# Attention head of an eight-stage kernel: the rotary halves change places by a matmul instead of DMAs, unit 1 is stacked later, key 0's parts are made on VectorE

## What is computed

```python
cq = _gelu(x @ wq + bq)
q_c = cq @ wqc + bqc
q_r = x @ wqr + bqr
ckv = _gelu(x @ wkv + bkv)
k_r = x @ wkr + bkr
k_c = ckv @ wkc + bkc
v = (ckv @ wv + bv)...
# x is the layer-normalised input; _apply_rope on q_r and k_r:
x1, x2 = (x[..., :d // 2], x[..., d // 2:])
rot = jnp.concatenate([-x2, x1], axis=-1)
return x * cos + rot * sin
...
q = _gelu(jnp.concatenate([q_c, q_r], axis=-1))...
k = _gelu(jnp.concatenate([k_c, k_r], axis=-1))...
scores = jnp.einsum('bhqd,bhkd->bhqk', q, k) * scale
...
attn = jax.nn.softmax(scores, axis=-1)
out = jnp.einsum('bhqk,bhkd->bhqd', attn, v)
return out @ wo + bo
```

## Time and profile before

| | |
|---|---|
| median of 3 runs | 4913.53 us (4904.8 to 4913.81) |
| the profiled execution | 4910.68 us |
| its span, first to last instruction | 4908.9 us |
| PE / DVE / ACT / POOL busy | 3882.5 / 2842.9 / 2210.7 / 2466.1 us |
| mean granted TensorE clock | 0.89 |
| the attention stage's head | about 3660 to 3910 us |
| attention's main loop | about 3910 to 4500 us |
| DMAs of the swap (s_crossed) | 16 of 256 KB, median 4.4 (query) and 3.7 us (key) from issue to landing |

### The profile page before, as it was taken

The page is one execution under the profiler, slowest core; times in us unless marked ns, Lnnn a source line. Parts: engine busy times, 40 slices in busy tenths (PEclk is TensorE's granted clock), DMA queues, the critical chain, the costliest instruction groups (busy, mean ns, idle before and its releaser), DMA issues.

```text
span 4908.9 us, 49219 instructions
## 1 busy us (share of the span) xinstructions
PE 3882.5 (79%) x15176; PEld 2243.6 (46%) x15178; DVE 2842.9 (58%) x4909; ACT 2210.7 (45%) x4071; POOL 2466.1 (50%) x2147
## 2 busy tenths in 40 slices
PE   6788888759956888797788869986875798888892
PEld 2333333347743556576334336654662233334571
DVE  5999999951126675211689952227333677664522
ACT  5665666521127775111566533333343355555241
POOL 5999999922212234211799944432455412222256
PEclk9999999959978999898789979996986699998896
DMA  5555655522210010221455521124156323321144
GB/s 154 159 160 162 160 155 160 154 72 75 101 54 17 18 35 27 96 95 63 136 162 159 150 92 45 45 71 125 57 151 129 108 41 45 45 32 55 39 141 132
DMA packets 311640, 476.06 MB, mean 97 GB/s; under 512 B 34762, under 2 KB 167606, under 8 KB 311306
## 3 DMA queue, kind: packets, MB, share of 16 engines
q1 hardware_dynamic: 276864, 388.61, 29.1%
q0 software_dynamic: 28992, 75.72, 5.4%
q10 hardware_dynamic: 5504, 8.39, 0.6%
HBM read 374.87 MB, written 97.10 MB: 96 GB/s over the span
## 4 chain that ended last, share of the span: by engine, by line
PE 37%; DVE 8%; issue 4%; ACT 4%; POOL 4%; DMA 3%; SPq 0%; DVEq 0%; ACTq 0%; POOLq 0%
PE s_gate_up L2325 8%; PE s_result_sum L2341 4%; PE s_hidden_sum L1761 3%; PE s_result_sum L1772 3%; PE s_out_sum L3696 3%; PE s_shared L2981 2%; PE s_scores L3637 2%; PE s_scores_T L3680 2%; DVE s_maxima L3328 2%; DVE s_decay L370 2%; PE s_shared L2991 1%; POOL s_gathered L1047 1%; PE s_transposed L2315 1%; PE s_mid_transposed L2334 1%; DVE s_h L377 1%
## 5 line engine op out<-in xcount | busy, mean ns | idle before, releaser
L435 POOL TENSOR_TENSOR s_h<-s_dtu,s_bc 128x1024 f32<-128x1024 f32 x384 | 902.5, 2359 | 48.9 <-PE s_y_sum L477 37.1
L477 PE MATMUL s_y_sum<-s_h,identity 128*128 128x512 f32 x1536 | 763.9, 635 | 133.4 <-POOL s_h L444 121.2
L402 ACT ACTIVATE s_decay<-s_dt,s_A 128x512 f32<-128x512 f32 x768 | 498.4, 682 | 309.1 <-DVE s_h L377 302.1
L477 PEld LDWEIGHTS s_y_sum<-s_h,identity 128*128 128x128 f32 x1536 | 292.8, 201 | 570.5 <-issue 291.0
L2325 PE MATMUL s_gate_up<-s_w_gate_up,s_rowsT 128*128 x1168 | 414.8, 487 | 1.7 <-issue 1.5
L3502 ACT ACTIVATE s_weights_T<-s_scores_T 128x1024 f32<-128x1024 f32 (+3 forms) x384 | 292.6, 811 | 260.0 <-PE s_scores_T L3680 258.3
L3328 DVE TENSOR_REDUCE s_maxima<-s_scores 128x1 f32<-128x512 f32 (+3 forms) x463 | 296.5, 658 | 187.2 <-PE s_scores L3641 104.3
L444 POOL TENSOR_TENSOR s_h<-s_h,s_bc 128x512 f32<-128x512 f32 x288 | 365.8, 1271 | 17.1 <-DVE s_h L370 12.4
L2384 DVE TENSOR_TENSOR s_mid<-s_act,s_gate_up 128x128 f32<-128x128 f32 (+1 forms) x225 | 91.5, 407 | 445.7 <-ACT s_act L2357 445.7
L3550 POOL TENSOR_SCALAR_AFFINE_SELECT s_weights_T<-s_weights_T 128x256 f32<-128x256 f32 x256 | 102.7, 406 | 472.2 <-ACT s_weights_T L3502 469.5
L370 DVE TENSOR_TENSOR_SCAN s_decay<-s_decay,s_carry,s_h 128x512 f32<-128x512 f32 x240 | 302.7, 1275 | 15.8 <-ACT s_decay L402 11.5
(11 more groups left out here) (533 smaller groups left out, 7644.7 us busy)
## 6 DMA issues: line engine op xcount, KB each, us to landing
s_bc<-s_bc_rows SPq DMA_DIRECT2D x384, 512.0 KB, 5.2
sorted_results<-s_result SPq DMA_DIRECT2D x158, 128.0 KB, 2.2
s_w_inter<-in_L_ffn_experts_inter SPq DMA_DIRECT2D x16, 1024.0 KB, 5.0
s_w_exp_out<-in_L_ffn_experts_out SPq DMA_DIRECT2D x16, 1024.0 KB, 7.9
s_queries<-parts_of_q SPq DMA_DIRECT2D x96, 128.0 KB, 4.9
s_keys<-parts_of_k SPq DMA_DIRECT2D x96, 128.0 KB, 8.0
results_by_token<-zeros SPq DMA_DIRECT2D x16, 512.0 KB, 5.9
s_pair<-results_by_token SPq DMA_DIRECT2D x16, 512.0 KB
```

The costliest lines, as they stand in the source:

```text
L402: S.e.activation(self.decay[:, (2 * g + d) % 4, :], dt[q // self.passes % 2][:, at, :], ACT.Exp, scale=A[:, at, g % ns:g % ns + 1]).then_i ...
L435: G.e.tensor_tensor(self.h[r][:], dtu[q // self.passes % 2][:, at:at + 2, :], mid(self.bc[r][:, 0, :], 2), ALU.mult).then_inc(*self.fed.up())
L477: made = T.e.matmul(self.y[:, d, :], ident[:], self.h[r][:, d, :], start=False, stop=g % ns == ns - 1)
```

## The change

- **Swap.** The DMAs on `crossed` are gone. A 128x128 matrix `halves`, the identity with its halves of columns exchanged, is written once by ScalarE into the tile of zeros, which nobody reads any more by then. A new step `change` on TensorE multiplies act1 by it, 512 columns at a time, into banks 3 and 4 of PSUM, and `cross` reads its crossed operand from there. Since these banks are also those of the transposes, a transpose waits for the crossing products (`crossed_made`) and the swap of a key for the copies of the transposes.
- **Ticks.** `CROSS` for the query moves from 35 to 36, the query's gelu from 39 to 40; in `cross` the sine products come before the cosine product.
- **Parts.** VectorE takes key 0 (`(0, 1)`) besides query 1, GpSimd keeps two of four activations.
- **Stacking.** Unit 1's halves are stacked after batch 1's and batch 2's stores.

```diff
-    w_c = H.sb("w_c", [P, P])
+    w_c, halves = H.sb("w_c", [P, P]), K.zeros[:, 0:P]
...
-    act_sum, rope_sum, roped, swapped = *K.events(3), K.event(32, "dma")
-    v_step, rope_added, values_sum, value_here = K.events(4)
+    act_sum, rope_sum, roped, swapped, halves_made = K.events(5)
+    v_step, crossed_made, rope_added, values_sum, value_here = K.events(5)
...
-    ROTATE, ROTATED, CROSS, ROTARY_MADE = ((28, 30), (36, 38)), ((29, 31), (37, 39)), (35, 43), (39, 47)
+    ROTATE, ROTATED, CHANGE = ((28, 30), (36, 38)), ((29, 31), (37, 39)), (33, 40)
+    CROSS, ROTARY_MADE = (36, 43), (40, 47)
...
-    turn_bank, latent_bank = lambda k: 3 + k, 5
+    turn_bank, latent_bank, crossed_bank = lambda k: 3 + k, 5, lambda c: 3 + c
...
-                if b == 0:
+                if ct == 0 and b == 0:
                     for a in range(2):
-                        stack(ct, a)
+                        stack(0, a)
+            if b in (1, 2):
+                stack(1, b - 1)
...
                 V.wait_ge(*weights_here.now())
-                V.wait_ge(*swapped.at(2 * b + j))
-                for i, (to, table) in enumerate(((act[1][j], cos), (crossed, sin))):
-                    V.e.tensor_tensor(to[:], to[:], table[:], ALU.mult).then_inc(*v_step.up())
-                    yield PERIOD * b + CROSS[j] + i + 1
+                for c in range(CPB):
+                    V.wait_ge(*swapped.at(4 * b + 2 * j + c))
+                    V.e.tensor_tensor(crossed[:, c * CH:(c + 1) * CH], bank[crossed_bank(c)], sin[:, c * CH:(c + 1) * CH],
+                                      ALU.mult).then_inc(*crossed_made.up())
+                yield PERIOD * b + CROSS[j] + 1
+                V.e.tensor_tensor(act[1][j][:], act[1][j][:], cos[:], ALU.mult).then_inc(*v_step.up())
+                yield PERIOD * b + CROSS[j] + 2
+                V.wait_ge(*crossed_made.now())
                 V.wait_ge(*v_step.now())
...
-            if (ct, j) != (1, 0):
+            if (ct, j) not in ((0, 1), (1, 0)):
                 return
...
+            for half in (HALF["q"], HALF["k"]):
+                made = S.e.activation(halves[:, half], K.ident[:, HALF["k" if half == HALF["q"] else "q"]], ACT.Copy)
+            made.then_inc(*halves_made.up())
...
-                S.wait_ge(*roped.now())
-                S.wait_ge(*rope_added.at(2 * b + j - 1))
-                for half in range(2):
-                    S.e.dma_start(crossed[half * DC:(half + 1) * DC, :],
-                                  act[1][j][(1 - half) * DC:(2 - half) * DC, :]).then_inc(*swapped.dma())
...
-            if (ct, j) == (1, 0):
+            if (ct, j) in ((0, 1), (1, 0)):
                 return
...
+        def change(b):
+            for j in range(2):
+                yield PERIOD * b + CHANGE[j]
+                T.wait_ge(*halves_made.at(0))
+                for c in range(CPB):
+                    T.wait_ge(*roped.at(4 * b + 2 * j + c))
+                    f = take(crossed_bank(c), crossed_made.at(4 * b + 2 * j + c))
+                    T.e.matmul(f, halves[:], act[1][j][:, c * CH:(c + 1) * CH], start=True, stop=True).then_inc(*swapped.up())
```

More of the change, by code:

```diff
@@ L3182, in head @@
             work += [(n, b) for n in ("gathers", "sums", "stats", "factors", "norm", "turn", "turned_rows", "latents",
-                                      "content", "rotate", "cross", "rotary")]
+                                      "content", "rotate", "change", "cross", "rotary")]
             work += [("split", (b, ct, j)) for ct in range(DT) for j in range(2)]
@@ L3723, in main @@
                 beside(2 * s + 1)
-        head(setup=setup, turn=turn, latents=latents, content=content, rotate=rotate, maxima=maxima, highest=highest,
+        head(setup=setup, turn=turn, latents=latents, content=content, rotate=rotate, change=change, maxima=maxima, highest=highest,
              values=values)
```

## The result

The change makes the kernel faster. Median of five runs 4881.41 us (4879.5 to 4889.6) against 4913.53 us (4904.69 to 4913.93, five runs); the ratio of the times is 0.9945, 95% interval 0.9934 to 0.9957, or 27 us of 4913.5. The medians lie further apart, 32.1 us, because two of the five runs before came at 4905 us and three at 4914; the means are 27.5 apart.

What follows compares the result with a forecast made beforehand. The head was taken as bound by a chain round ScalarE, GpSimd and VectorE, beside DMA waits. Terms -13.7 +0.5 -3.0 +1.1 +0.4 = -14.7 from 4910.7 gave 4896 us, range 4882 to 4908.

Steps and rivals of the forecast that it cites:

- Batch 0, query half: Attention's head: VectorE's aggregate no longer waits for the swap, so ScalarE's normalisation comes 4.3 us earlier.
- Batch 0, key half: Swapping matmuls replace the DMA wait; aggregate 1.9 us earlier at the low clock, 6.2 for batch 0 together.
- Loads 13.7 us earlier, store of query 1 landing 13.7 earlier: Unit 0's loads start earlier through key 0 on VectorE; store duration unchanged; 13.7 us, batch 0's 6.2 contained.
- its other road: Batch 1: ScalarE's cast reached through the add waiting for gathered rows, not query 1's store; ready near 3755.
- Batch 1, key half: Cold TensorE runs the pair and latent matmuls in a row: 0.5 us more.
- Batch 2, query half: VectorE's aggregate loses the cosine product ahead, 1.2 us, and blocking by GpSimd, 2.0: 3.0 us less taken.
- Batch 2, key half: A low-clock pair and a score take TensorE to 3841.1 against 3839.96: 1.1 us more.
- Rival (3): Extra matmuls raise TensorE's clock in the head, about 12 us more gain: 4884 us; chance 0.12.
- Batch 3: Packed TensorE adds 1.9 us for the query pair, less blocking saves 1.5: 0.4 us more.
- (1): Only batch 0's gain stays, 6.2 us instead of 13.7, as query 1's store otherwise lands late: 4903.5 us; chance 0.12.
- (4): Nothing gained: gathers and GpSimd hold the round and each microsecond won is waited away, 4911 us; chance 0.09.
- (2): TensorE becomes the bound, eight pairs at 3.62 us all in the chain: 4921.5 us; chance 0.07.

Runs made afterwards that it cites:

- the second profiles: The unchanged kernel and the full change, each timed and profiled once more: ratios 1.0005 and 0.9947, heads 236.0 and 209.5 us.
- The ticks alone: Kernel before with only the query's cross at tick 36 and gelu at 40, swap still by DMA: ratio 0.9992, head 225.1 us.
- the pairs alone: Kernel before, swap by DMA kept, with the eight pairs of swapping matmuls added on TensorE, results unread: ratio 1.0014, head 233.4 us.
- the doubled pairs: Kernel with the change and every swapping matmul done twice, 16 more of 128x512: ratio 0.9968, head 213.9 us.
- old stacking: Kernel with the change, but unit 1 stacked after batch 0's rotary stores again, 24 loads in one piece: ratio 0.9950, head 205.8 us.

## Why the prediction was right in direction and short in size

The undoings don't add up (8 for key 0's parts, 8 for the ticks, 1 for the swap, nothing for the stacking), but a path from before to the change does: ticks -11.4 us, swap on TensorE -7.7 on top, key 0's parts -11.6 on top, later stacking +3.2. The last lies in batch 0, and the swap's 7.7 hold the same 3 us, so the swap is nearer to 5 there. Once all the rest is in place it is worth 1 to 2 us: with the ticks changed, little stands behind its wait. So the swap itself is the smaller part of the gain.

- *Batch 0, query half: 4.3 us.* Right in number, by luck in the last link. ScalarE's normalisation came 3.9 us earlier (5.3 between the second profiles). The aggregate came 6.0 earlier, and GpSimd, as I had said, first ended its gather. But its factors were then done in 1.9 us, at 3712.45, where I had 3.4 to the normalisation. ScalarE normalised only at 3714.31, because its copy of act0q stood ahead (3713.72), and that waited for content matmuls which came 2.2 us later in the head than before. I had called their delay hidden by ScalarE's idle time. In the second profile ScalarE did wait for GpSimd.
- *Batch 0, key half: 1.9, 6.2 together.* The fourth aggregate came 7.9 us earlier (7.8 in the second profile). Right within 2 us, though the pair took 2.16 us and not the 3.6 that I had put in.
- *Loads 13.7 us earlier, store of query 1 landing 13.7 earlier.* The first half holds: 11.9 for the load, 12.8 for the store's issue. The step that failed is "I let them and the store behind them take as long as now". From the first load to ScalarE's cast it took 33.8 and 32.2 us before, 24.9 and 26.6 with the change. With a faster drain I had put the whole term at 16.5 us at most and given the rest to the swaps' DMAs; it was 20.9 in this profile and 17 to 20 in the second. Those DMAs held the engines for 2.8 us of before's stretch, but the changed kernel with the swap by DMA holds them too and takes 26.2 us, so they are not what separates it from before. What does is who makes key 0's parts: 24.8 to 27.4 us in the seven profiles where VectorE does and the wait can be read, 29.1 to 33.8 in the six where GpSimd does. "The store still ends last" failed with it: ScalarE stood 0.48 and 2.05 us for the store, not 4 to 7, and the cast went 20.9 us earlier, about when I had its other road ready (3755.1 on before's scale, against "near 3755"). The windows of the load stretch (columns as in the earlier trace rows), before, with key 0 on GpSimd, and after:

```profile
3742.20:3776.00 33.80, 11.34 (x24) 4.61 (x22) 9.66 (x20) 7.18 (x12) 16.83 (x15) 0.67 1.04 189
```

```profile
3739.60:3769.00 29.40, 10.12 (x27) 4.20 (x25) 11.53 (x21) 7.06 (x11) 15.31 (x15) 0.74 1.04 199
```

```profile
3740.90:3765.80 24.90, 11.35 (x29) 4.72 (x28) 13.67 (x24) 9.38 (x16) 16.28 (x15) 0.77 1.03 232
```

  The DMA engines are full in all three, and move 189, 199 and 232 GB/s. The last two stretches carry nearly the same bytes (rate times length, 5.9 and 5.8 MB). By queue, the gathers took 6.3 us of all engines in both, 1.24 and 1.36 MB; the loads and stores on SyncE's queue took 24.2 us for 4.61 MB with key 0 on GpSimd and 19.4 us for 4.42 MB with the change. So it is the loads and stores that went faster for their bytes; why was not settled.
- *Batch 1, key half: 0.5 more.* 0.3 less: the sixth aggregate has 21.2 us, the cast 20.9. In the second profiles it is 2.1 less (19.5 and 17.4). Small, as I had said, but not more.
- *Batch 2, query half: 3.0 less.* 3.4. Right.
- *Batch 2, key half: 1.1 more.* Wrong in sign: 4.1 us less. The step that failed is that I left ScalarE's order and the clock as they were and counted only the pair. The ticks alone, without any pair, take this half from 26.5 to 23.1, since the gelu no longer stands ahead of the copy that the latent matmuls wait for; I had put nothing for the gelu's tick. The swap itself costs time here, as forecast: 22.1 and 22.8 us with it, 20.3 with the DMAs in its place. With the change the pair does fill TensorE's stop, and the latent matmuls take 1.88 instead of 3.78 us, but with the new ticks they take 1.98 and 1.99 without it too. Rival (3), the clock, has its mechanism shown, not its price. The time of the change, 4881, is nearer to its 4884 than to my 4896; the stretches don't put 12 us down to added matmuls, and the pairs alone bring the head 3. The Trainium skill, "TensorE: Matmul & The Clock Gate", Part 1, has the clock follow recent activity. The pairs alone agree, with 1.88 us behind two of three added pairs where 3.5 to 3.8 stood.
- *Batch 3: 0.4 more.* 0.3. Right.

The Trainium skill, "SBUF — State Buffer", section "SBUF: two separate sides": the lock-out cuts as the rule says in one direction, 3.71 us for a subtraction of 1.22 beside GpSimd's of 2.13. The other direction, by which the sum would have been 4906, costs little: GpSimd's factors of batch 0's key half took 1.11, 1.07 and 1.13 us with the change and 1.11, 0.33 and 1.25 before, 0.6 us more, and in no other half did they take longer than before.

Rivals (1) and (4) fall with the 28 us, (2) with the doubled pairs. Of my three signs that I am wrong, one came up: VectorE stood 2.18 us for TensorE's swap in batch 0's key half. It was a bad sign: VectorE had stood idle 12.15 us there before, and stands 2.01 for the DMAs when they take the swap's place in the changed kernel. The other two didn't: the first load came 11.9 us earlier, and attention's loop changed only as it does without any change.

## What to carry to other kernels

Before a slow transfer is replaced, look at what stands behind the instruction that waits for it: two ticks, which moved an aggregate ahead of the wait on one engine and a gelu behind a copy on another, took 11 us off this head, and the transfer's own replacement then brought 1 to 5. When an instruction is moved for one engine's sake, look at every engine whose order moves with it: batch 2's key half became 3.4 us shorter with the ticks alone, and no term of the sum stood for it. Where a store queues behind a batch of loads, its landing can move by more than its issue, so take its duration as a range, from full engines to empty ones. When the code outside a stage is untouched and a kernel's times still differ by 10 us, compare the stage's own length from a fixed instruction to a fixed instruction.

## What the hardware showed that I had not expected

- A stop of the same length was followed by either clock. The higher one held over stops of 1.47 us (ticks alone) and 2.41 us (old stacking), and was gone after 2.35 and 5.12 us in the two profiles of the change (fences above). Before's batch 2 had it until the 2.40 us stop ahead of the earlier trace rows's latent matmuls and lost it there, with a granted clock of 1.00 ahead of the stop, 0.50 behind it:

```profile
3836.90:3837.60 0.70, 0.50 (x3) 0.21 (x3) 0.66 (x3) 0.27 (x1) 0.00 (x0) 1.00 0.00 0
3839.90:3841.00 1.10, 1.04 (x2) 0.52 (x3) 0.00 (x0) 1.10 (x3) 0.00 (x0) 0.50 0.47 160
```

- With full DMA engines (share 1.03 to 1.04) nearly the same 5.8 MB of loads, stores and gathers moved at 199 or 232 GB/s.
- Attention's loop, with the same instructions, took 580.4, 580.5, 582.6 to 585.7 or 592.0 us. Two profiles (pairs alone, pairs doubled) agree to 0.1 us in the start of each unit. The clock over its first 580 us is 0.99 where it took 580.4, and 0.97 where it took 592.0 (the change, then the pairs doubled):

```profile
3892.16:4472.16 580.00, 517.69 (x3691) 221.14 (x3689) 389.45 (x714) 319.04 (x442) 121.80 (x270) 0.99 0.24 35
```

```profile
3888.54:4468.54 580.00, 519.19 (x3616) 220.81 (x3615) 388.07 (x711) 310.08 (x431) 119.58 (x264) 0.97 0.24 35
```
